# Placing the edges of a graph kernel: TensorE turns the one-hots of the table lookup, ScalarE no longer makes them from broadcast rows, and the lookup has two PSUM banks in place of four

## What is computed

```
h   = relu([x[dst'], x[src'] - x[dst']] @ W + b); out = segment_max(h, ...)
x   = layernorm(x + max(out, 0))
deg = segment_sum(ones, col);  norm = deg^-0.5[row] * deg^-0.5[col]
tx  = segment_sum(norm * tx[col], row)      # five times, result += coeffs[k] * tx
x   = layernorm(x + result)
```

## Time and profile before

| | |
|---|---|
| time, median of 3 runs | 4285.44 us (4284.15 to 4291.22) |
| profiled execution | 4285.35 us, span 4283.3 us |
| placing stage in the trace | from about 740 us to 1328.4 us |
| batches, instructions on the span | 98 batches, 63707 instructions |
| mean granted TensorE clock over the span | 0.675 |

### The profile page before, as it was taken

How to read it: one execution, slowest core, us unless ns; L and a number is a source line. 1 busy time by engine, 2 the same in 40 slices (tenths; PEclk the granted TensorE clock), 3 DMA queues, 4 the chain that set the end, 5 groups by cost and what they waited for, 6 DMA issues and landing times. The chain is left out here.

```text
span 4283.3 us, 63707 instructions
## 1 busy us (share of the span) xinstructions
PE 2044.9 (48%) x10071; PEld 1187.5 (28%) x10071; DVE 2726.5 (64%) x8453; ACT 1594.1 (37%) x3952; POOL 2846.3 (66%) x2750
## 2 busy tenths in 40 slices
PE   7995554888886666647774444433322221000000
PEld 5773343555553322224441111111100000000000
DVE  8997789999995555539995444444432222006999
ACT  7996574777773333323441111111100000121222
POOL 5664453677775777756666777766677777775666
PEclk9998888999996555559996555555555555555555
DMA  3215552555555444427773444433211111005665
GB/s 102 76 21 176 170 146 78 154 157 159 160 155 163 130 133 138 135 79 216 220 220 81 80 80 79 77 70 70 68 36 34 34 35 31 22 22 148 203 206 172
DMA packets 466910, 485.82 MB, mean 113 GB/s; under 512 B 305147, under 2 KB 317409, under 8 KB 466883
## 3 DMA queue, kind: packets, MB, share of 16 engines
q1 hardware_dynamic: 377326, 372.57, 30.2%
q0 software_dynamic: 76800, 87.29, 9.4%
q10 hardware_dynamic: 12756, 25.69, 1.7%
HBM read 248.31 MB, written 242.90 MB: 115 GB/s over the span
## 5 line engine op out<-in xcount | busy, mean ns | idle before, releaser
L1279 PE MATMUL zT_H<-ident,z_H 128*64 128x128 f32 x816 | 247.6, 407 | 886.6 <-issue 676.9
L893 POOL DMA_INDIRECT rec<-rec_sb,pos x392 | 405.6, 1035 | 226.3 <-issue 159.0
L1157 POOL DMA_INDIRECT rows_H<-tab,at_H x416 | 401.9, 966 | 173.1 <-issue 114.2
L1083 POOL DMA_INDIRECT node_max<-back_M,to_M x400 | 407.9, 1020 | 157.4 <-issue 119.7
L1167 POOL DMA_INDIRECT node_sum<-back_H,to_H x400 | 398.1, 995 | 121.8 <-issue 121.8
L1157 POOL DMA_INDIRECT rows_H<-x,at_H x400 | 377.5, 944 | 136.0 <-issue 117.7
L1235 DVE SCALAR_TENSOR_TENSOR value_H<-rows_H,coef 128x128 f32<-128x128 f32 x208 | 73.6, 354 | 517.3 <-DMA rows_H<-tab,at_H 517.3
L1423 POOL TENSOR_TENSOR res_n<-cent_n,rstd_n 125x640 f32<-125x640 f32 x160 | 231.4, 1446 | 174.4 <-DVE rstd_n L1507 94.1
L1279 PEld LDWEIGHTS zT_H<-ident,z_H 128*64 128x64 f32 x816 | 74.5, 139 | 952.4 <-issue 952.4
L826 PE MATMUL gps<-table,hiT 125*128 125x400 bf16 x1568 | 303.1, 337 | 59.3 <-DVE picked L761 58.2
L1415 POOL TENSOR_TENSOR cent_n<-y_n,mean_n 125x640 f32<-125x640 f32 x160 | 246.6, 1541 | 127.4 <-DVE mean_n L1495 127.4
(11 more groups left out here) (236 smaller groups left out, 6504.8 us busy)
## 6 DMA issues: line engine op xcount, KB each, us to landing
tab<-zeros SPq DMA_DIRECT2D x32, 802.0 KB
tab<-zeros_M SPq DMA_DIRECT2D x32, 802.0 KB
tab<-Xt SPq DMA_DIRECT2D x400, 64.0 KB
hibc_f<-dst_hi_rows SPq DMA_DIRECT2D x98, 256.0 KB
hibc<-hi_rows SPq DMA_DIRECT2D x98, 256.0 KB
srcbc<-src_rows SPq DMA_DIRECT2D x98, 256.0 KB
node_max<-fill SPq DMA_DIRECT2D x50, 500.0 KB
node_sum<-zeros_M SPq DMA_DIRECT2D x50, 500.0 KB
```

The lines of the kernel that those rows point to most:

```text
L893: pool.indirect_dma_start(out=d.rec, out_offset=bass.IndirectOffsetOnAxis(ap=pos[:, s, j:j + 1], axis=0), in_=rec[:, s, j, :], in_offset=N ...
L1083: pool.indirect_dma_start(out=d.node_max, out_offset=bass.IndirectOffsetOnAxis(ap=to[:, s, j:j + 1], axis=0), in_=back[:, s, j, :], in_off ...
L1157: pool.indirect_dma_start(out=rows[:, s, j, :], out_offset=None, in_=gather, in_offset=bass.IndirectOffsetOnAxis(ap=at[:, s, j:j + 1], axi ...
L1279: last = pe.transpose(zT[s][:, j * P:(j + 1) * P], z[:, s, j, :], k.ident[:])
```

## The change

The broadcast of the high parts and the three ScalarE instructions that made `hiT` from it go. In their place TensorE multiplies each tile's `ohp`, which VectorE has made anyway, with a bf16 identity matrix (`one`): the product is the one-hot turned, in a new PSUM tile `hps` of two banks. ScalarE copies it to `hiT` with one instruction. The 8 PSUM banks are `tps` 4, `hps` 2, so 2 are left for the lookup: tile j uses bank j % 2. `turn` for batch n+1 stands in TensorE's program after the lookup of batch n and before its adds. The last two batches are written out behind the loop.

```diff
-            hibc, srcbc = isb("hibc", [P, 2, GPOS]), isb("srcbc", [P, 2, GPOS])
-            dist = isb("dist", [NP, 2, GPOS])
+            srcbc = isb("srcbc", [P, 2, GPOS])
+            one = isb("one", [P, P], BF16)
-            gps = [inner.enter_context(nc.psum_tensor(f"gps{j}", [P, BANK], FP32)) for j in range(4)]
+            gps = [inner.enter_context(nc.psum_tensor(f"gps{j}", [P, BANK], FP32)) for j in range(2)]
+            hps = inner.enter_context(nc.psum_tensor("hps", [NP, 2, BANK], FP32))
...
-                        before, twice = settle(sp, k, i, i * 2)
+                        before, = settle(sp, k, i)
                         sp.wait_ge(rows_used[s], before)
-                        sp.wait_ge(dist_done[s], twice)
-                        for to, of in ((hibc, d.hi_rows), (srcbc, d.src_rows)):
-                            sp.dma_start(to[:, s], of[ds(i * GPOS + s * (ET // 2 * P), GPOS)].partition_broadcast(P)
-                                         ).then_inc(rows_in[s], 16)
+                        sp.dma_start(srcbc[:, s], d.src_rows[ds(i * GPOS + s * (ET // 2 * P), GPOS)].partition_broadcast(P)
+                                     ).then_inc(rows_in[s], 16)
...
-                        dve.scalar_tensor_tensor(picked[:, j], gps[j][:, 0:NR], 1.0, ohc[:, s, j],
+                        dve.scalar_tensor_tensor(picked[:, j], gps[j % 2][:, 0:NR], 1.0, ohc[:, s, j],
...
+                def turn(i, s):
+
+                    pe.wait_ge(onehots[s], i + 1)
+                    pe.wait_ge(hiT_ready[1 - s], i + s)
+                    for j in range(4):
+                        for h in range(2):
+                            last = pe.matmul(hps[:, h, j * P:(j + 1) * P], ohp[:, s, j, h::2], one[:], start=True, stop=True)
+                    last.then_inc(turned[s], 1)
...
-                            pe.wait_ge(got_read[j], i * 2 + s)
+                        pe.wait_ge(got_read[(j + 2) % 4], i * 2 + s + j // 2)
...
+                    high_part(s, 0)
+                    if ahead:
+                        turn(i + s, 1 - s)
...
                 def rows(i, s):
 
-                    act.wait_ge(rows_in[s], i * 32 + 32)
-                    act.wait_ge(hiT_ready[1 - s], i + s)
-                    for h in range(2):
-                        act.activation(dist[:, h], hibc[0:NP, s], ACT.Abs, bias=part[0:NP, h:h + 1]
-                                       ).then_inc(dist_done[s], 1)
-                    act.wait_ge(dist_done[s], i * 2 + 2)
+                    act.wait_ge(turned[s], i + 1)
                     act.wait_ge(added[s], i)
-                    act.activation(hiT[:, s], dist[:], ACT.Relu, bias=1.0, scale=-1.0).then_inc(hiT_ready[s], 1)
+                    act.activation(hiT[:, s], hps[:], ACT.Copy).then_inc(hiT_ready[s], 1)
```

More of the change, by code:

```diff
@@ L685, in count_and_place @@
         two = lambda name: [sem(f"{name}{s}") for s in range(2)]
-        rows_in, rows_used, dist_done, hiT_ready = two("rows_in"), two("rows_used"), two("dist_done"), two("hiT_ready")
+        rows_in, rows_used, turned, hiT_ready = two("rows_in"), two("rows_used"), two("turned"), two("hiT_ready")
         onehots, added, table_ready = two("onehots"), two("added"), two("table_ready")
@@ L691, in count_and_place @@
         seeded, high_ready, low_left = sem("seeded"), two("high_ready"), two("low_left")
+        one_ready = sem("one_ready")
         lch = sem("lch")
@@ L733, in ranks @@
                 def ranks(i, s):
-                    dve.wait_ge(rows_in[s], i * 32 + 32)
+                    dve.wait_ge(rows_in[s], i * 16 + 16)
                     for j in range(4):
@@ L812, in _ @@
                 last.then_inc(seeded, 1)
+                pe.wait_ge(one_ready, 1)
+                turn(0, 0)
                 pe.wait_ge(high_ready[0], 1)
                 high_part(0, 1).then_inc(low_left[0], 1)
-                with pe.Fori(0, EB // 2) as i:
-                    for s in range(2):
[L817 to L822, removed]
-                            pe.wait_ge(got_read[j], i * 2 + s)
-                            for h in range(2):
[L825 to L835, removed]
@@ new lines, in batch @@
+                def batch(i, s, ahead=True):
+                    pe.wait_ge(hiT_ready[s], i + 1)
+                    pe.wait_ge(table_ready[s], i + 1)
+                    for j in range(4):
+                        if j == 2:
+                            pe.wait_ge(high_ready[1 - s], i + s + 1)
+                            high_part(1 - s, 1).then_inc(low_left[1 - s], 1)
+                        pe.wait_ge(got_read[(j + 2) % 4], i * 2 + s + j // 2)
+                        for h in range(2):
+                            for w in range(2):
+                                last = pe.matmul(gps[j % 2][:, 0:NR], hiT[:, s, h, j * P:(j + 1) * P], table[:, s, w, h],
+                                                 start=h + w == 0, stop=h + w == 2)
+                        last.then_inc(got[j], 1)
+                    high_part(s, 0)
+                    if ahead:
+                        turn(i + s, 1 - s)
+                    for j in range(4):
+                        for h in range(2):
+                            last = pe.matmul(tps[s][:, h, 0:NR], ohp[:, s, j, h::2], ohc[:, s, j],
+                                             start=False, stop=True, skip_group_check=True)
+                    last.then_inc(added[s], 1)
@@ L837, in _ @@
+                with pe.Fori(0, LAST) as i:
+                    for s in range(2):
+                        batch(i, s)
+                batch(LAST, 0)
+                batch(LAST, 1, ahead=False)
             @block.scalar
@@ L864, in low @@
                     act.activation(table[:, s, 1], tps[s][:, :, 0:NR], ACT.Copy).then_inc(table_ready[s], 1)
+                act.activation(one[:], k.ident[:], ACT.Copy).then_inc(one_ready, 1)
                 for sign in range(2):
```

## The result

The changed kernel takes 4363.27 us, median of 4 runs (4360.48 to 4367.88). The kernel before took 4288.15 us beside it (4 runs, 4284.15 to 4291.22). The ratio is 1.0177, with an interval of 1.0159 to 1.0194. The prediction said 4355 us, slower, with 4335 to 4405 as its range.

What follows compares the result with a forecast made beforehand. VectorE, with no idle time left, was taken to bound the placing stage. Two banks add 96 x 0.70 = 67 us, the start 3, together 70 on 4285.35: 4355 us, 1.6% slower, with 4335 to 4405 for 8 in 10 runs.

Steps and rivals of the forecast that it cites:

- VectorE waits for no DMA: Placing stage: removing ScalarE's two |h - p| and SyncE's 98 broadcasts frees nothing on the path; priced at nothing.
- Two banks: VectorE's picks in placing: third waits 0.53 us, fourth 0.18, for later lookups; 0.70 us a batch, bounded by 0.5 and 0.8.
- The turn: TensorE's eight turning matmuls ahead of the adds: T of 0.5 to 0.83 us, taken as 0.7, hidden by 0.1.
- the predicted cover of 0.83: Before VectorE's one-hots at P+4.64: adds ready at P + 3.81 + T, so T is hidden up to 0.83 us.
- the rule: Placing step if the turn outlasts what hides it: 5.60 + T us, each further tenth of T on the path.
- ScalarE's copy: Late copy to `hiT`, low table behind it: lookups there at P+5.9 and P+6.6, needed at P+6.43 and P+6.92; hidden.
- Four banks alone would not save the change: Loop through copy, low table, lookup, put back and turn: 5.4 + T = 6.1 us, under 6.43 but over the old 5.73.
- Start and end: Placing stage: 3 us more at the start for the first `hiT`; at the end GpSimd's last scatters hide the waits.
- Idle 0.53 and 0.18 us, near 67 in all: Sign of being right: VectorE idle before third and fourth picks for TensorE's gps, near 67 us in all.
- The clock: Rival: TensorE's clock falls to 1.2 GHz in placing and TensorE becomes the bound, about 4770 us; chance 0.07.
- Picks did not get shorter with the DMAs gone: Rival: without 25 MB of broadcasts VectorE's instructions shrink, 4285 us or somewhat below; chance 0.07, of which 0.04 faster.
- A long turn: Rival: turning matmuls take T = 1.33 us, step 6.93, 4403 us; chance 0.18.

Runs made afterwards that it cites:

- The kernel with three banks: Changed kernel with the turning matmuls as bf16 transposes into one PSUM bank, leaving three banks for the lookup: 4308.87 us, ratio 1.0044 to the kernel before.
- the loop shortened by ScalarE's order: Changed kernel with three lookup banks and transposes, ScalarE making the low table ahead of the copy to `hiT`: 4296.57 us, ratio 1.0020 to the kernel before.
- the other trace of before: Kernel before, unchanged, profiled once more: 4284.21 us, mean step 5.84 us.
- the kernel with three turns: Changed kernel with each turning matmul done three times over, same result: 4429.36 us in its second run, ratio 1.0330 to the kernel before.
- the last experiment: Changed kernel with three banks, transposes and low table first; ScalarE makes high one-hots of tiles 0 and 1 in place of VectorE: 4269.34 us, ratio 0.9957.

## Why the prediction was right

- **What bounds the stage.** VectorE had 3 us of slack in 540, and what was put in its way came out in the time. 1.4 us of ScalarE's work for each batch and the broadcasts went away for nothing. One reading was wrong: "VectorE waits for no DMA". Its `positions` waited three times for a scatter, 1.0 us in all, and six long steps hang on these waits.
- **Two banks**, 0.70 us a batch. The two pick times, P+1.51 and P+2.18, were P+1.52 and P+2.20. Shown to be the cause: the two banks alone cost 67 us, and a third one takes most of it back, with the turn or without.
- **The turn**, T = 0.5 to 0.83, taken as 0.7: T is 1003.44 - 1002.96 = 0.48 us, just below the lower bound. Apart, the matmuls stand (0.64 - 0.22) / 7 = 0.06 us from each other; the line between rows of 50 and 400 columns had given 0.064. So the 40 ns put on for the slow weight load were wrong: the load of 138 ns is wholly hidden. The Trainium skill's 104 ns for 125 columns (TensorE: Matmul & The Clock Gate, LDWEIGHTS) sets no pace here; T by it was, as an estimate, to be 0.83. 0.48 and the 0.7 of the sum both lie under the predicted cover of 0.83, and no wait before the one-hots shows. The cover itself was smaller than predicted in half of the batches: the adds' signal can reach VectorE at 1003.44 + 1.52 + 0.15 = P+4.48, and VectorE comes to `ohp` at P+4.86 in this batch and P+4.67 in the others, so that a turn of up to 0.86 and 0.67 us is hidden. That "hidden, by 0.1" held is in part luck: T = 0.7 would have brought a wait of 0.03 us in every second batch, and T = 0.83 a step above 6.43, by the rule with 0.19 added 6.62.
- **ScalarE's copy** was hidden, as predicted. The next lookups start at 1005.63 behind the low table, so the first four matmuls are through at about P+5.9, the predicted time, and the next pick comes at P+6.64. The 83 waits of the picks are one for each batch, the third pick's; no first pick waits.
- **"Four banks alone would not save the change"**, since the loop through the turned copy is 5.4 + T. With T = 0.48 that is 5.88. The kernel with three banks had 5.99, against 5.88 with the loop shortened by ScalarE's order. For three banks the claim holds by 0.1 us only, and the shorter loop is a change of two lines. Four banks with the turn were not run.
- **Start and end.** 3 us were taken for the start, 3.0 were measured (up to 4.4 against the other trace of before). With ScalarE's order changed the start was 2.6 us shorter (14.8 to 12.25), more than the 1.5 us between the two traces of before, so most of it was the first copy standing ahead of the table copies, one of the three reasons given. The end was priced at nothing and cost 1.7.
- **What was missed.** The loop's edge on VectorE, 9 us, and in the other direction the uneven steps of before, 6.5 us. The sum used the undisturbed step of 5.73 for before, where the mean was 5.80. The two nearly cancel, which is luck, so 4355 against 4363 is better than its terms.
- **The signs.** "Idle 0.53 and 0.18 us, near 67 in all" was badly put: the third pick's bracket says 0.45, the fourth has none, and the page counts 60.5 us for all picks, since the short accumulator rows cover part of the delay. The start times of the rows were the right thing to name.
- **The rivals.** The clock stayed at 1.00. (The prediction put it at half for all of the time behind placing; slices 18 to 20 of the earlier trace rows are 9s, in a later stage that the change does not touch.) Picks did not get shorter with the DMAs gone (570 ns). A long turn is what the kernel with three turns has; its T was 1.43 and its time 4429, where the rival had T = 1.33 and 4403.

## What to carry to other kernels

When an engine without slack reads PSUM banks that another fills, count how many fills can be done ahead of its first read: here each of the banks taken away was priced by the fill's train and two handoffs, 0.70 us a batch for the second and 0.04 for the first. Work taken off an engine that waits was worth something here only when its free time was used to take work off the one that doesn't, as the last experiment did. When an operation is made later by a change, look at which copies stand behind it in its engine's order, and swap those that can go first.

## What the runs showed of the hardware

- A short loop (two batches in a body) costs VectorE 0.19 us per turn in all kernels in which a pick comes late in every batch, even by 0.04 us. In the kernel before it costs nothing in nearly all turns; the three exceptions, 0.13 to 0.19 us, come right behind waits of VectorE, one of them in the rows below, from the trace before. That it is hidden otherwise by instructions fetched or queued ahead is argued, not shown.

```profile
938.31 0.57 DVE L761 SCALAR_TENSOR_TENSOR picked<-gps,ohc 128x400 bf16<-128x400 f32 x1 [0.75 <-PE gps L826]
...
939.00 0.35 DVE L738 SCALAR_TENSOR_TENSOR eq<-srcbc,recs,mask 128x128 bf16<-128x128 f32 x1
```

- A body of eight batches cost about 6.3 us per jump in this kernel, with 44 packets on the instruction queue in 500 us, where the changed kernel had none.
- Matmuls of 128 bf16 columns with 125 strided weight columns follow each other every 0.06 us, 8 in 0.64 us and 24 in 1.60, though a load of such weights takes 138 ns.
- A signal from TensorE's last result to another engine took 0.04 us for ScalarE's copy and 0.15 for VectorE's wait on the adds, by the ends that the profile gives for matmuls. On one chip, where the kernel before took 4776 us, the same signal to the copy took 0.6 and 1.8 us, as medians, in two of the kernels. Why it did is open.
